# Attention scores written to device memory in three pieces per sequence instead of seven

## What is computed

```python
q, k, v = (x @ Wq), (x @ Wk), (x @ Wv)          # 16 heads of 64
k, v = concat(mem_k, k), concat(mem_v, v)        # 4 memory keys ahead
dots = einsum('bhid,bhjd->bhij', l2norm(q), l2norm(k)) * QK_SCALE
dots = einsum('hg,bgij->bhij', W_pre_th, dots)   # mix over heads
dots = where(causal, mask_value, dots)
vk = top_k(dots, 64)[0][..., -1:]
attn = softmax(where(dots < vk, mask_value, dots))
attn = einsum('hg,bgij->bhij', W_post_th, attn)  # mix over heads again
out = einsum('bhij,bhjd->bhid', attn, v) * head_scale_params
out = (out * sigmoid(x @ Wg + bg)) @ Wo
```

## Time and profile before

| | us |
|---|---|
| median of 3 runs | 3675.55 |
| lowest, highest | 3673.79, 3677.22 |
| the profiled execution | 3675.17 |
| its span in the trace | 3673.9 |
| granted TensorE clock, mean over the span | 0.978 of 2.4 GHz |

### The profile page before, as it was taken

One profiled execution on the slowest core, in us unless ns is written; L12 is line 12 of the kernel. 1 busy time (PEld: TensorE's weight loads), 2 busy tenths in 40 slices (PEclk: granted clock), 3 DMA queues, 4 the chain that ended last, 5 costly groups with the idle time before them and its releaser, 6 DMA issues.

```text
span 3673.9 us, 79012 instructions
## 1 busy us (share of the span) xinstructions
PE 3446.7 (94%) x19551; PEld 2576.0 (70%) x19551; DVE 3405.5 (93%) x18541; ACT 3091.2 (84%) x10773; POOL 1742.8 (47%) x3672
## 2 busy tenths in 40 slices
PE   5999999996899999999999999999999999999987
PEld 4888888883576666666666666666666666676665
DVE  7888888854999999999999999999999999999994
ACT  6777777756799899999999999989999999999964
POOL 0000000003566666666666666666666666666663
PEclk8999999996899999999999999999999999999999
DMA  3000000002222222222222222222222222222220
GB/s 131 13 12 12 13 12 12 8 8 71 63 65 76 70 66 71 73 81 76 65 65 65 64 66 65 74 72 67 70 74 76 81 65 65 65 65 66 63 63 4
DMA packets 254141, 210.76 MB, mean 57 GB/s; under 512 B 78000, under 2 KB 234736, under 8 KB 252912
## 3 DMA queue, kind: packets, MB, share of 16 engines
q1 hardware_dynamic: 253680, 205.70, 18.0%
HBM read 93.97 MB, written 111.67 MB: 56 GB/s over the span
## 4 chain that ended last, share of the span: by engine, by line
PE 46%; DVE 33%; ACT 8%; POOL 6%; issue 5%; DMA 1%; SPq 0%; DVEq 0%; ACTq 0%; POOLq 0%
DVE W L1766 12%; PE bank L363 11%; DVE last L1787 8%; PE bank L221 8%; PE bank L1348 4%; PE bank L1363 3%; PE bank L331 3%; PE bank L1375 3%; PE bank L1440 3%; ACT T L1543 2%; PE bank L195 2%; POOL below L1913 2%; DVE last L1785 2%; ACT SN L1559 2%; PE bank L400 2%
## 5 line engine op out<-in xcount | busy, mean ns | idle before, releaser
L1766 DVE MATCH_REPLACE8 W<-last,W 128x130 f32<-128x130 f32 (+17 forms) x3456 | 880.4, 263 | 0.0
L1787 DVE MAX8 last<-W 128x8 f32<-128x130 f32 (+17 forms) x3456 | 771.5, 266 | 0.0
L1872 POOL TENSOR_SCALAR posts<-post,share 128x128 f32<-128x128 f32 x1024 | 361.4, 371 | 345.9 <-DVE share L1696 345.9
L1543 ACT ACTIVATE T<-T,peak 128x260 f32<-128x260 f32 (+15 forms) x1024 | 417.2, 435 | 46.4 <-POOL T L1923 43.3
L886 DVE TENSOR_TENSOR_SCAN hs<-dA,dx 128x256 f32<-128x256 f32 x512 | 352.0, 688 | 86.1 <-issue 80.1
L1363 PE MATMUL bank<-T,pre 128*128 128x40 f32 (+15 forms) x1024 | 373.1, 447 | 35.4 <-ACT T L1567 26.8
L1559 ACT ACTIVATE SN<-bank,rq 128x260 f32<-128x260 f32 (+1 forms) x1024 | 360.5, 431 | 46.7 <-PE bank L1348 29.1
L1923 POOL TENSOR_TENSOR T<-T,below 128x520 f32<-128x520 f32 (+12 forms) x416 | 360.1, 882 | 24.0 <-DVE below L1796 8.6
L1375 PE MATMUL bank<-posts,T 128*128 128x128 f32 (+7 forms) x2048 | 303.5, 284 | 10.3 <-POOL posts L1872 9.2
L1363 PEld LDWEIGHTS bank<-T,pre 128*128 128x128 f32 x1024 | 168.2, 193 | 200.3 <-ACT T L1567 98.9
L1375 PEld LDWEIGHTS bank<-posts,T 128*128 128x128 f32 (+7 forms) x2048 | 242.7, 171 | 91.6 <-issue 44.9
(11 more groups left out here) (244 smaller groups left out, 9494.6 us busy)
## 6 DMA issues: line engine op xcount, KB each, us to landing
scores_by_token<-SN SPq DMA_DIRECT2D x64, 520.0 KB, 2.6
scores_by_token<-SN SPq DMA_DIRECT2D x64, 396.0 KB, 3.1
scores_by_token<-SN SPq DMA_DIRECT2D x32, 780.0 KB, 3.3
scores_by_token<-SN SPq DMA_DIRECT2D x32, 264.0 KB, 2.6
scores_by_token<-SN SPq DMA_DIRECT2D x32, 260.0 KB, 2.1
T<-scores_by_token SPq DMA_DIRECT2D x32, 244.0 KB, 3.1
T<-scores_by_token SPq DMA_DIRECT2D x32, 228.0 KB, 3.3
T<-scores_by_token SPq DMA_DIRECT2D x32, 212.0 KB, 3.9
```

Source lines behind the costliest of these rows:

```text
L1543: act.activation(one, one, ACT.Exp, bias=peak[k % 2][:, j:j + 1], accum_out=total[k % 4][:, j:j + 1]).then_inc(e_made, 1)
L1766: dve.match_replace(both[:, s, at:to], best[n], both[:, s, at:to], LOWEST).then_inc(ranked, 1)
L1787: dve.max(best[n], both[:, s, at:to]).then_inc(ranked, 1)
L1872: pool.tensor_scalar(posts[(4 * k + j) % NP][:], post[:], share[k % 2][:, j:j + 1], 1.0, ALU.mult, ALU.mult).then_inc(posts_made, 1)
```

## The change

One line: the table of pieces. Block 0 is written in one piece of 16 heads once all six score pieces are kept. Block 1 is written in two, ten heads after ten pieces and six heads after all sixteen.

```diff
-STAGES = [[(0, 6, 2), (6, 12, 4), (12, 16, 6)], [(0, 6, 6), (6, 10, 10), (10, 14, 14), (14, 16, 16)]]
+STAGES = [[(0, 16, 6)], [(0, 10, 10), (10, 16, 16)]]
```

## The result

The changed kernel takes 3840.91 us (median of 4 runs, 3837.51 to 3846.68), the kernel before beside it 3674.67. The ratio is 1.0454, with a 95% interval of 1.0441 to 1.0467: 166 us slower, 5.2 us per sequence. The forecast was 3765 us with 3705 to 3800. The sign was right; the size was short by almost half.

The account below looks back on a forecast made before the run. The prediction took a slack-free chain through the DMAs to VectorE's L1744 as the bound. Stalls of 1.8 (block 0) and 1.0 us (block 1) over 32 sequences added 89.6 us to 3675.17, giving 3765 us, range 3705 to 3800.

Parts of the forecast that it names:

- What bounds the kernel: Attention phase: VectorE's wait at L1744 ends a chain through the DMAs without slack, so added delay is paid every sequence.
- The half of block 0: Block 0's single 1056 KB write lands 2.7 us later; less 0.9 us slack, TensorE stalls 1.8 us at the first premix.
- The bound of 3.0: Upper end for the extra landing time of block 0's large write, 3.0 us, from six steps of 0.5 us.
- the 2.7 us of the plateau: Block 0's extra landing time for 1056 KB over 264 KB, from some 300 GB/s plus 1.7 us fixed.
- (d): Block 0's large write takes 7 us or more to land: 4.5 us per sequence, 3820 us; chance 0.08.
- the sum on record: Both blocks' TensorE stalls, 1.8 + 1.0 = 2.8 us per sequence, 89.6 us over 32 sequences.
- Block 1: Last write of 780 instead of 260 KB lands 1.2 us later; less 0.2 us slack, 1.0 us of TensorE stall.
- Edits at nothing: Four fewer DMA issues per sequence, dropped or moved ScalarE waits and block 1's later first write change nothing.
- (a): Only block 1 is paid, block 0's stall being worked off before the last scores: 3707 us; chance 0.12.
- (b): Not slower: TensorE's 3.5 us free per period takes the stall and L1744 keeps its place: 3675 us; chance 0.05.
- (c): Faster by larger pieces: fixed DMA parts fall away and VectorE gains its 0.35 us wait: 3664 us; chance 0.03.
- The second sign of being wrong on record: The prediction is wrong if VectorE's wait at L1744 grows by less than TensorE's wait does.

Follow-up runs that it names:

- The two filled kernels: Unused matmuls put into TensorE's stall at block 0: three on the changed kernel, 3803.87 us; two on the kernel with block 0 in two 8-head writes, 3746.82 us.
- the five writes: Kernel before, with block 0 written as twelve and four heads and block 1 as ten, four and two: 3686.93 us, ratio 1.0034.
- block 0 alone: Kernel before, with block 0 written in one piece of 16 heads and block 1 left in its four pieces: 3814.27 us, ratio 1.0382.
- two halves: Kernel before, with block 0 in two writes of 8 heads, both issued when all 16 are kept, block 1 unchanged: 3789.02 us, ratio 1.0311.

## Why the prediction was wrong

**What bounds the kernel.** Half right. The stretch is hung on L1744, with 42.3 to 42.8 us from it to the next first copy in every kernel whose marks were taken, and so a delay is paid in every sequence, as the part on the bound says. Wrong was the step "a wait that occurs in all 29 periods says that this chain has no slack at all". VectorE did wait for GpSimd's mask each time, but the mask waited for GpSimd, which was behind its own list by 0.70 us, and not for TensorE. The row of the chain showed it: L1888 x4 is four masks of block 0 ahead of the one that counts.

**The half of block 0.** The direction, the place and the slack of 0.9 us were right. The term "1.8 us of stall" was mis-sized: the first premix came 3.2 us later. The landing came out at 6.7 us for 5.3, and 4.1 - 0.9 is 3.2, so the slack was right to the tenth. I took the 2.7 us of the plateau over the 3.0 of the step from 264 to 396 KB; the landings of 660 and 990 KB lie on or above the latter, and the merged form adds 0.4. The bound of 3.0 did not take this in, though rival (d) did, with 7 us to land.

**Nothing for the clock.** This is the step that is missing. Sixteen matmuls of L221 were named as what stands behind the stall, and their duration was taken as given. Behind an average stall of 2.6 us or more they ran at half speed in most sequences: 1.6 to 1.8 us per sequence, 52 to 56 us of the 166. The two filled kernels, 37 and 42 us faster with more work, show that the cause is TensorE's standing still; the second does so with the DMAs unchanged. The Trainium skill has the rule (TensorE: Matmul & The Clock Gate, Part 1): after standing idle, TensorE is held at half its clock until it has been busy again for a time; the trace agrees behind 22 of 28 stalls, of 2.9 to 3.8 us at the weight loads, and not behind the other six, of 2.9 to 3.6 us. The trace of before has half-speed stretches too, in 17 us of 2500, so the forecast could have priced it. With the landing at 6.7 us and no clock the sum on record gives 3.2 + 1.0 per sequence, 134 us; the clock adds 56, GpSimd's 0.6 per sequence gives back 19, and 5 us are left without an account. By the same numbers the kernel without the clock's part would be near 3790 us, inside the range: it is the missing term that put the time outside.

**Block 1.** The landing (3.3 for 2.1 us) and TensorE's stall (0.9 for 1.0) were right. The period rose by 0.3 to 0.5 us, since GpSimd's lead hid the rest. The phrase "with nothing behind it that could take it back but VectorE's own wait" is the one that failed.

**Edits at nothing.** These held: ScalarE waits for no DMA in the changed kernel either, and four issues fewer brought nothing that can be seen.

**Rivals.** (a) got the wrong block: block 0 is paid and block 1 mostly isn't. (b) fell with the row of 42.5 us. (c) fell with the five writes, which were slower. (d) is nearest in time, 3820 us, and its mechanism, a landing of about 7 us, is half of what happened; the half speed was in none of them, so that the nearness of its time is in part luck. What was to be seen at L1744, 3.2 us of wait, was 1.0 (1.3 with `issue`), because most of VectorE's waiting came out elsewhere in the period. The second sign of being wrong on record did come: the wait at L1744 grew by 17 us in 1000 to 3500 us, and the weight loads' wait for the loads by 112, from 7.6 to 120.0. VectorE's busy time, forecast as unchanged, rose by 26 us over the whole, which no run here explains.

## What to carry to other kernels

When data goes out in pieces and a wait is for all of them, only the piece issued last sets the end: keep it small, and keep the queue ahead of it short enough that it isn't held up. Fewer and larger pieces saved nothing measurable here, and grew the last one. Price a stall of TensorE twice, once for the wait and once for what runs behind it at half speed; here 0.8 us was free of that and 2.6 us wasn't, and waits of 1.0 to 2.5 us at other places brought it now and then. And where the bound engine waits for a helper, look whether the helper was itself late, before its other inputs are called critical.

## What the runs showed of the hardware

- The granted clock of TensorE went to half (1.2 GHz) behind stalls that were 2.6 to 3.4 us on average in a stream that had been at full speed, in most sequences but not in all: 22, 27 and 26 of 28 in the changed kernel, with block 0 alone and with two halves. Two neighbours with stalls of 3.6 and 3.6 us at the weight loads took 88.6 and 91.5 us. Stalls of 0.8 us at this place never brought it; waits of 1.9 us at L1429 did in five of the 29 sequences of before. Matmuls whose result is not used, put into the stall, kept the clock up.
- A write whose two outer dimensions merge to 2048 rows is slower than the same bytes kept as 128 x 15 and 128 x 1: 6.3 us against 5.9 for all of it, with 519 ns of issue instead of 387. The write of one head issued right behind 990 KB held SP for 1448 ns.
- The time of a write to landing, for runs of 528 bytes, was 2.6, 3.1, 4.1 and 5.6 us for 264, 396, 660 and 990 KB; with runs of 2080, 4160, 6240 and 10400 bytes (block 1), 2.1, 2.6, 3.3 and 4.5 us for 260, 520, 780 and 1300 KB.
